# A mixture-of-experts block with a linear-attention layer before it on one Trainium2 core: the first turn of the mix in an order of its own, expert scaling in the even turns, last subtractions and the list read moved

## What is computed

```python
x = x + _L0_xattn_ref(w, u, _layernorm(x), ctx_2048)      # wkv: a scan over time, per channel
#   y[t] = (A p + E v[t]) / (A q + E);  p = A2 p + E2 v[t];  q = A2 q + E2
x = x + _L0_ffn_ref(_layernorm(x), ...)
#   probs = softmax(x @ gate_w.T); top 2 of 8 experts, by their probabilities (comb)
#   moe_out = sum_e comb[t, e] * (silu(x @ Wg[e].T) * (x @ Wu[e].T)) @ Wd[e].T     # inner size 256
#   sh = sigmoid(x @ shared_expert_gate_w.T) * shared expert of inner size 1024
#   x + moe_out + sh
```

## Time and profile before

| | us |
|---|---|
| median of 3 runs | 570.06 |
| lowest and highest | 569.88 and 572.94 |
| the profiled execution's own time | 573.75 |
| its span | 570.1 |
| PE busy in the span | 493.4 |
| DVE busy in the span | 423.6 |
| POOL busy in the span | 342.1 |
| ACT busy in the span | 276.4 |

### The profile page before, as it was taken

One profiled execution on the slowest core, in us unless ns is written; L12 is line 12 of the kernel. 1 busy time (PEld: TensorE's weight loads), 2 busy tenths in 40 slices (PEclk: granted clock), 3 DMA queues, 4 the chain that ended last, 5 costly groups with the idle time before them and its releaser, 6 DMA issues.

```text
span 570.1 us, 10205 instructions
## 1 busy us (share of the span) xinstructions
PE 493.4 (87%) x2703; PEld 264.5 (46%) x2703; DVE 423.6 (74%) x954; ACT 276.4 (48%) x534; POOL 342.1 (60%) x421
## 2 busy tenths in 40 slices
PE   1116699899999999999999979899999999999970
PEld 1113345445555555455555544355545555555530
DVE  5778987999989899899898876466656665566650
ACT  4849837475674764756746433433323333333310
POOL 5767946757848578579485364315465665565432
PEclk9999989999999999999999999899999999999995
DMA  7960104115213223052101410305566866576352
GB/s 288 413 259 19 38 18 185 57 27 178 76 56 131 76 103 138 21 185 75 38 20 39 131 60 14 112 20 113 99 108 123 157 114 115 109 127 120 72 75 37
DMA packets 25929, 59.14 MB, mean 104 GB/s; under 512 B 6314, under 2 KB 6314, under 8 KB 24338
## 3 DMA queue, kind: packets, MB, share of 16 engines
q0 software_dynamic: 9824, 20.90, 20.7%
q1 hardware_dynamic: 16050, 37.59, 18.3%
HBM read 37.83 MB, written 20.65 MB: 103 GB/s over the span
## 4 chain that ended last, share of the span: by engine, by line
PE 54%; DVE 14%; issue 11%; POOL 6%; DMA 6%; ACT 5%; SPq 1%; POOLq 0%; DVEq 0%; ACTq 0%
PE GU L882 30%; PE DN L897 14%; DMA out<-wall,idsa 5%; PE XT L827 3%; PE HT L827 3%; ACT wall L700 3%; DVE st L1080 2%; DVE wall L1077 2%; DVE wall L1070 2%; DVE hb L1194 1%; POOL nrm L409 1%; DVE th L1191 1%; DVE xb L1095 1%; SPq L365 1%; POOL xb L572 1%
## 5 line engine op out<-in xcount | busy, mean ns | idle before, releaser
L882 PE MATMUL GU<-wall,xt 128*128 128x512 f16 x768 | 187.9, 385 | 2.1 <-DVE wall L1172 2.0
L897 PE MATMUL DN<-wall,hx 128*128 128x512 f16 (+1 forms) x618 | 151.8, 382 | 6.4 <-DVE hx L1199 4.5
L882 PEld LDWEIGHTS GU<-wall,xt 128*128 128x128 f16 x768 | 75.7, 101 | 70.3 <-issue 4.0
L582 POOL DMA_INDIRECT out<-wall,idsa x39 | 61.8, 1584 | 73.2 <-SPq L369 35.2
L657 ACT ACTIVATE hx<-HT 128x256 f16<-128x256 f32 x103 | 39.0, 379 | 134.3 <-PE HT L827 132.6
L897 PEld LDWEIGHTS DN<-wall,hx 128*128 128x128 f16 x618 | 60.4, 99 | 82.7 <-issue 8.1
L1199 DVE TENSOR_TENSOR hx<-HT,hx 128x256 f16<-128x256 f32 x103 | 43.1, 418 | 65.9 <-ACT hx L657 55.5
L652 ACT ACTIVATE th<-GU,scl 128x256 f32<-128x256 f32 x103 | 48.4, 470 | 77.9 <-PE GU L882 74.9
L882 PE MATMUL GU<-wall,kb 128*128 x240 | 61.4, 379 | 0.2 <-DVE kb L1373 0.2
L572 POOL DMA_INDIRECT xb<-xn_rows,idsi x39 | 40.2, 1030 | 33.1 <-DMA out<-xb 15.6
L882 PE MATMUL GU<-wall,xnb 128*128 x228 | 58.5, 379 | 0.6 <-DVE xnb L1373 0.6
(11 more groups left out here) (162 smaller groups left out, 755.3 us busy)
## 6 DMA issues: line engine op xcount, KB each, us to landing
wall<-wgu SPq DMA_DIRECT2D x12, 1024.0 KB, 9.8
wall<-wd SPq DMA_DIRECT2D x12, 512.0 KB, 10.4
out<-xb SPq DMA_DIRECT2D x20, 256.0 KB, 2.3
xb<-x SPq DMA_DIRECT2D x16, 256.0 KB, 2.8
cb<-ctx_t SPq DMA_DIRECT2D x16, 256.0 KB
xn_rows<-xnb SPq DMA_DIRECT2D x16, 256.0 KB
xb<-xn_rows,idsi POOLq DMA_INDIRECT x39
out<-wall,idsa POOLq DMA_INDIRECT x39
```

Source lines behind the costliest of these rows:

```text
L582: pool.indirect_dma_start(out, bass.IndirectOffsetOnAxis(ap=idsa[:, j:j + 1], axis=0), ye[j % RESULTS], None, compute_op=ALU.add).then_inc ...
L882: ins = nc.tensor.matmul(GU[par][:], lhs(xp, c), gate_up(base, wp, c), start=m == 0, stop=m == 3 * HC - 1)
L897: ins = nc.tensor.matmul(DN[:], hx[par][:, hp * IE + c * P:hp * IE + (c + 1) * P], down(base, wp, c), start=start and m == 0, stop=stop an ...
```

## The change

1. A first turn of its own. Behind the preparation, each engine has a hand-written stretch for tile 2's mixing and the shared units 0 to 3, and `turns` starts at turn 3. In it POOL has `norm(1, 1)`, the four `shared_d_lo` and `quotient(2)` in another order, ACT takes each `shared_d_split(s)` and the squares of expert 0 behind the activations of the units, DVE divides the reciprocals, and PE takes unit 0 before the transposes of tile 1's result. The transposes of tile 2's result (`y_back(2)`) are taken in turn 3, between units 4 and 5.
2. `SQUARED_IN` is 2, 4, ..., 14. Expert 0 gets its first four pieces in turn 3 and the other two in turn 4, its scales in turn 3 and its subtractions in turns 4 and 5, as all others do. Expert 6 now has all six pieces at the end of turn 15 on ACT.
3. Expert 6's first two subtractions stand on POOL before `norm(15, 1)`, the third behind the read of the lists.
4. The lists' cast stands on DVE before `hidden_lo(60)`, their transpose on PE in unit 61, before its last six products.
5. The mask and the two constant matrices of `ranks` are float16 (`tri16`, `all16`); one more memset makes them.

The core of the diff (left out: the tiles and the lines of DVE and ACT that only leave turn 2 for the new stretches):

```diff
-SQUARED_IN = [2] + list(range(3, 2 * E - 2, 2))
+SQUARED_IN = list(range(2, 2 * E, 2))
...
             def other_consts():
-                link(pool.affine_select(out=tri[:], in_=ones[:], compare_op=ALU.is_gt, fill=0.0,
+                link(pool.memset(all16[:], 1.0))
+                link(pool.affine_select(out=tri16[:], in_=all16[:], compare_op=ALU.is_gt, fill=0.0,
                                         base=0, pattern=[[1, P]], channel_multiplier=-1))
                 link(pool.iota(toki[:], [[P, B], [0, LW]], base=0, channel_multiplier=1))
...
             scales(1, SHARED)
             norm(2, 0, agg1, norm1, k_rdy)
             quotient(1)
-            norm(3, 0, agg1, norm1, k_rdy)
             first_product(2)
             second_product(2)
+            norm(3, 0, agg1, norm1, k_rdy)
+
+            norm(1, 1, agg2, norm2, xn_rdy)
+            shared_d_lo(0)
+            shared_d_lo(1)
+            shared_d_lo(2)
+            norm(4, 0, agg1, norm1, k_rdy)
+            first_product(3)
+            second_product(3)
+            shared_d_lo(3)
+            quotient(2)
             def turn(i, j, sq_e, hi_e, ws_e, lo_e):
                 if i >= 4:
                     scatter(i - 4)
                 pool.wait_ge(nd, i + 1)
-                if i >= 3:
-                    pool.wait_ge(masked, (i - 2) * 2)
-                if lo_e == 0:
-                    expert_lo(0, 0)
+                pool.wait_ge(masked, (i - 2) * 2)
                 if lo_e is not None:
                     expert_lo(lo_e, 1)
-                if i == LAG:
-                    shared_d_lo(0)
                 norm(i - 1, 1, agg2, norm2, xn_rdy)
-                if i == LAG:
-                    shared_d_lo(1)
                 if lo_e is not None:
                     expert_lo(lo_e, 2)
-                if ws_e:
+                if ws_e is not None:
                     expert_lo(ws_e, 0)
                 if i + 2 < B:
                     norm(i + 2, 0, agg1, norm1, k_rdy)
-                if i == LAG:
-                    shared_d_lo(2)
-                    shared_d_lo(3)
+                if i == LAG + 1:
+                    scales(2, 0)
                 if i + 1 < B:
                     first_product(i + 1)
                     second_product(i + 1)
...
                 if sq_e is not None:
                     scales(sq_e + 2, sq_e)
-            turns(turn, LAG)
+            turns(turn, LAG + 1)
+            expert_lo(E - 2, 0)
+            expert_lo(E - 2, 1)
             norm(B - 1, 1, agg2, norm2, xn_rdy)
             scatter(B - 4)
-            expert_lo(E - 2, 1)
-            expert_lo(E - 2, 2)
             for t in range(B - 3, B):
                 scatter(t)
...
             pool.wait_ge(scattered, TOPK * B * 16)
             pool.indirect_dma_start(ids_back, None, ids_tiles,
                                     bass.IndirectOffsetOnAxis(ap=listi[0:NSLOT, 0:1], axis=0)).then_inc(ids_ld, 16)
+            expert_lo(E - 2, 2)
             scales(E + 1, E - 1)
...
             gu_square(3)
+            d_square(3)
             second_norm(0)
-            d_square(3)
             act_hi(0)
             shared_gu_hi(0)
             first_norm(2)
             shared_gu_hi(1)
+            shared_gu_hi(2)
             both_exps(2)
-            shared_gu_hi(2)
+
+            unit_tanh(0, 0, SHARED)
+            router_out(0)
             shared_d_split(0)
+            unit_hi(0, 0)
             first_norm(3)
             shared_gu_hi(3)
+            unit_tanh(1, 1, SHARED)
+            second_norm(1)
+            shared_d_split(1)
+            unit_hi(1, 1)
+            unit_tanh(2, 0, SHARED)
+            act_hi(1)
+            both_exps(3)
+            shared_d_split(2)
+            unit_hi(2, 0)
+            first_norm(4)
+            unit_tanh(3, 1, SHARED)
+            shared_d_split(3)
+            for k in range(3):
+                expert_square(0, k)
             def turn(i, j, sq_e, hi_e, ws_e, lo_e):
                 n = j * SU
...
                 if hi_e is not None:
                     for k in range(4):
                         expert_piece(hi_e, k)
-                if hi_e == 0:
-                    expert_piece(0, 4)
-                    expert_piece(0, 5)
-                elif ws_e:
+                if i == B - 1:
+                    ws_e = hi_e
+                if ws_e is not None:
                     expert_piece(ws_e, 4)
                     expert_piece(ws_e, 5)
-            turns(turn, LAG)
+            turns(turn, LAG + 1)
...
                 pe.wait_ge(lg_rdy, t + 2 if routed is None else routed)
-                nc.tensor.matmul(LG[:, 16:16 + E], tri[:], mask[:], start=True, stop=True)
-                nc.tensor.matmul(LG[:, 16 + E:16 + 2 * E], ones[:], mask[:], start=True, stop=True).then_inc(ranked, 1)
+                nc.tensor.matmul(LG[:, 16:16 + E], tri16[:], mask[:], start=True, stop=True)
+                nc.tensor.matmul(LG[:, 16 + E:16 + 2 * E], all16[:], mask[:], start=True, stop=True).then_inc(ranked, 1)
...
             keys_t(2)
-            y_back(1)
+
+            def first_turn(u):
+                if u == 0:
+                    router(0, 2)
+                    y_back(1)
+                if u == 1:
+                    keys_t(3)
+                if u == 2:
+                    xn_t_(1)
+
+            shared_units(0, first_turn)
             def turn(i, j, sq_e, hi_e, ws_e, lo_e):
...
-                        router(i - 2, 2 + sum(a < i for a in SQUARED_IN))
+                        router(i - 2, 2 if i == LAG + 1 else 2 + sum(a < i for a in SQUARED_IN))
+                        if i == LAG + 1:
+                            y_back(i - 1)
                         if i + 1 < B:
                             keys_t(i + 1)
+                    if u == 1 and i == LAG + 1:
+                        sum_squares(2, 2 * SU + 4, i - 1)
                     if u == 2:
                         xn_t_(i - 1)
-                        if i >= 3:
-                            ranks(i - 3)
+                        if i == LAG + 1:
+                            pe.wait_ge(sq_red, 3)
+                        ranks(i - 3)
                         if sq_e is not None:
                             sum_squares(sq_e + 2, sq_e * 3 + (2 * SU + 4), i - 1)
                 shared_units(j, beside)
                 y_back(i)
...
-            def last_steps(u):
-                if u == 1:
-
-                    pe.wait_ge(ids_f, 1)
-                    nc.tensor.transpose(KT[:, 0:NSLOT], ids_float, ident[0:NSLOT, 0:NSLOT]).then_inc(ids_t, 1)
+            def lists_t():
+
+                pe.wait_ge(ids_f, 1)
+                nc.tensor.transpose(KT[:, 0:NSLOT], ids_float, ident[0:NSLOT, 0:NSLOT]).then_inc(ids_t, 1)
             shared_units(B - LAG, last_of_mix, between={0: third_last_ranks},
                          beyond={1: last_router, 2: last_ranks})
-            shared_units(B - LAG + 1, last_steps, beyond={3: lambda: gathered_t(0, 0)})
+            shared_units(B - LAG + 1, beyond={1: lists_t, 3: lambda: gathered_t(0, 0)})
             def expert_of(j):
...
             act_lo(0)
-            reciprocals(1, 0, HC)
+            reciprocals(1, 0, 2)
             shared_gu_lo(0)
-            first_stats(3)
+            reciprocals(1, 2, 2)
             keys(2)
             shared_gu_lo(1)
+            first_stats(3)
             dve.wait_ge(consts, CONSTS)
+
+            hidden(0, 0, SHARED)
+            residual_and_stats(1)
+            shared_gu_lo(2)
+            hidden_lo(0, 0)
+            scan_e(2)
+            hidden(1, 1, SHARED)
+            shared_gu_lo(3)
+            scan_ev(2)
+            hidden_lo(1, 1)
+            hidden(2, 0, SHARED)
+            add_now(2)
+            act_lo(1)
+            keys(3)
+            reciprocals(2, 0, 2)
+            hidden_lo(2, 0)
+            first_stats(4)
+            hidden(3, 1, SHARED)
+            reciprocals(2, 2, 2)
+            dve.wait_ge(scale_step, 2 * SCALE_STEPS + 1)
+            nc.vector.tensor_scalar(half_y[:], scale(SHARED, YINV), 0.5, None, ALU.mult).then_inc(half_rdy, 1)
+            dve.wait_ge(half_rdy, 1)
+            small_steps(t=0)
             def turn(i, j, sq_e, hi_e, ws_e, lo_e):
                 n = j * SU
...
             experts_of_slots()
-            hidden_lo(n, 0)
-            hidden(n + 1, 1, SHARED)
-            accumulate(B - 2)
             dve.wait_ge(ids_ld, 16)
             nc.vector.tensor_copy(ids_float.unsqueeze(2), ids_back.rearrange("r (p a) -> r p a", a=LW)[:, :, 0:1]
                                   ).then_inc(ids_f, 1)
+            hidden_lo(n, 0)
             dve.wait_ge(ids_t, 1)
             nc.vector.tensor_copy(idsi[:], KT[:, 0:NSLOT]).then_inc(ids_rdy, 1)
             dve.wait_ge(pads_rdy, 1)
             TT(idsa[:], KT[:, 0:NSLOT], pad_of[:], ALU.add).then_inc(ids_rdy, 1)
+            hidden(n + 1, 1, SHARED)
+            accumulate(B - 2)
             hidden_lo(n + 1, 1)
             hidden(n + 2, 0, SHARED)
```

34 lines of the change are left out of this document (11 added, 23 removed).

## The result

The changed kernel takes **574.68 us** (median of 20 runs, 573.76 to 576.19) beside 571.70 us of the kernel before in the same series (20 runs; 570.06 was the median of its first three). The ratio is **1.0047**, 95% interval 1.0028 to 1.0065: 2.7 us slower, where 568.0 was forecast, 0.4% faster. (The forecast started from 570.06; the 1.6 us up to 571.70 are in its distance to 574.68, but not in the ratio.) Its profiled execution has a span of 573.5 us (570.1 before).

The account below looks back on a forecast made before the run. PE was taken as the bound, busy 493 of 570 us. The terms +1.7 - 3.7 - 0.6 - 1.0 + 2.6 + 1.8 - 2.8 = -2.0, put on the median 570.06, gave 568.0 us; range 562.5 to 574.0.

Parts of the forecast that it names:

- the one on the turns: Turns 4 to 15: PE is the bound, so float16 ranks save 0.31 us a tile, 3.7 in all.
- Turn 4: Turn 4 becomes as long as turn 5 with expert 0's pieces and subtractions spread: 3.1 us gained.
- Turn 15: Turn 15: two ACT pieces before it instead of four end PE's waits for DVE; 1.0 us gained, bounds 0 and 1.0.
- The first turn: Start to turn 4: its products come 4.8 us later, at 98.2; less turn 4's 3.1, a cost of 1.7.
- The walk: Step-by-step timing of the new first turn, DVE's scans held until the quotient is over: y(2) at 80.5, turn 4's products at 98.2.
- Behind the turns: After turn 15: PE stands 6 us before unit 57; 2.6 us lost, plus 1.8 for a clock fall.
- The list read: At the lists: PE's wait of 2.37 and 1.8 of slow clock go, waits of 0.5 and 0.9 come; 2.8 us gained.
- The third subtraction: Before `hidden_lo(59)`: it stands in the way of small DVE steps with some 2 us of room; costs nothing, otherwise 2.1.
- The slots: The 39 expert slots: not touched, 0 us.
- Of the rivals the second: DVE's backlog is carried on: turns 4 and 5 are each 3.1 us longer, 574.2 us in all; chance 0.21.
- my signs of being wrong: Turn 4 starting before 95, turns 5 to 14 not 0.3 shorter each, or the wait before unit 57 under 4.

Follow-up runs that it names:

- PE kept busy: The changed kernel with 48 repeated products put into PE's waits in the first turn; ratio 1.0051 to the kernel before.
- the three repairs of the new turn: The changed kernel with unit 2's down split earlier on ACT (1.0029), three queues reordered (1.0042), or PE repeating products in its waits (1.0051), against the kernel before.
- the two parts run alone: The kernel before with only the float16 ranks (ratio 0.9919), and the kernel before with only the list read moved (ratio 0.9968).

## Why the prediction was wrong

The forecast was -2.0 on the span and +3.4 came. By its own steps:

- **The step that failed first is the one on the turns**: "That is PE's own work ..., so there only what leaves PE counts." In turns 4 to 15 the ranks gave 2.4 instead of 3.7, since POOL's quotient is the end of every second turn. The sign of it was in the trace of before: six products take 1.3, yet the group begun at 227.94 was followed by the transposes at 229.55 only, 0.3 of waiting that falls under the size at which the timeline names a wait. On top of that the new pattern has one such turn more (5 to 13 instead of 6 to 12), and turn 5 took 19.83 in this profile, where eight of the nine other profiles with this order of the turns have 19.3: turns 5 to 14 are 1.05 longer than with the ranks alone (189.71 against 188.66), about half of it for each. The two make 2.4 of the error.
- **Turn 4: right**, 3.2 for 3.4. **Turn 15: half**: it is 0.55 shorter than with the ranks alone (18.21 against 18.76), forecast 1.0; the ranks gave 0.62 there for the 0.31 forecast, so the line of the table comes out nearly right by luck.
- **The first turn: right in direction, 2.0 too small.** The walk put y(2) at 80.5; it came at 84.75. Two terms were mis-sized. Some 2.3 is the lower clock behind the rests before units 2 and 4, which the walk did not have (with PE kept busy y(2) came at 82.44). Some 1.8 is the quotient: the walk held DVE's scans until it was over, but the first scan began with it and it was the quotient's two steps that took 2.25 and 1.03. (The walk's own last step isn't clear either: 75.6 and the steps named, 1.86, 2.13 and 1.42, give 81.0 and not 80.5.) From y(2) to turn 4's products the walk had 17.7 and 15.5 came, which took half of the miss back. None of the three repairs of the new turn gave back the 7 us: in their profiles they moved the wait and gave 3.2, 0.4 and 0.
- **Behind the turns: right in every link**, 4.75 for 3.8 with the ranks: the wait was 6.31 for 6.0, and the fall behind it cost about 2.4 (6.0 us from 338.05 to 344.08, 3.6 at full speed) for the 1.8 taken from the one at the lists. A clock fall stands in this term and another in the list read's, and they were never two: of before, after and the two parts run alone each profile shows one fall behind turn 15, at one wait or another.
- **The list read: 1.0, forecast 2.8.** The 1.8 for the clock was booked as removed with its wait; it came back at the router's wait of 3.07 in the run that had the list read alone. **The third subtraction: 0.98, forecast 0**; its bound of 2.1 stood in the text, but DVE's step beside it grew by 2.4 (2.61 for 0.18), more than the "some 2 us of room". The 1.68 of the table is these parts together: 1.0 and 1.69 of clock, less 0.98.
- **The slots: forecast untouched, 1.17 gained.** About 0.7 of it are two waits for DVE at the same instructions: 0.56 and 0.94 before and in every profile with the old first turn, 0.21 and 0.61 after and in every one with the new; the rest is in one DMA wait that varies from profile to profile (0 to 1.3). Why is open; no run bears on it.

Of the rivals the second (turns 4 and 5 as long as the old turn 4, 574.2) has the time that came, by another way: turns 4 and 5 were 19.05 and 19.83. Of my signs of being wrong the one on turns 5 to 14 came true; the other two, turn 4's start (100.22) and the wait before unit 57 (6.31), did not.

What is **shown**: the new first turn costs 7 us and the old one gives them back; POOL's four subtractions are not the whole cause (without them 4.7 of the 7.1 stay by the runs), and keeping the clock up in the first two rests doesn't shorten it, because it falls at the next. The head start of unit 0 alone is worth nothing in the old order, because unit 2 doesn't hang on it: in the old order it waits for DVE's third scaling until 57.7, in the new one for POOL's first subtraction until 57.1. What is **open**: how much of the 7 us is the subtractions' and how much the clock's (the falls of the new turn moved y(2) by 2.3), and which chain makes the rest of the new turn (57.14 to 99.73 on PE, 42.6 us) longer than the old (57.72 to 92.94, 35.2 us). The row that differs most is POOL's quotient of tile 2, at 81.32 and at 70.68; but with that mended it was another. I take it that DVE, POOL and ACT together are full there, by their work and by holding each other up, and that each order hides a different part; that is argued, not shown.

## What to carry to other kernels

A stretch in which no wait is listed can still have a second engine 0.3 us behind the first: subtract the work from the distance of two rows before booking a gain per turn, and ask who is next. In these profiles a slow stretch of the clock belonged to a region with several rests and not to one wait: take its cost out of the sum only when all of these rests go, and compare two orders of a turn only with the fall at the same place. And before moving a step to the head of a stretch, ask what the second and third step behind it hang on: unit 0 started 2.5 us earlier and unit 2 only 0.6.
